# Feed-forward layer with 4-bit weights: the down projection's weights are prepared beside the gate and up products and kept in DRAM

## The reference

```python
w = stack([W_q >> 4 & 15, W_q & 15])               # two nibbles per word
w = (w - zero) * scale                             # one zero and scale for 64 inputs
x = x + layernorm(attention(layernorm(x)))
h = silu(layernorm(x) @ Wg.T) * (layernorm(x) @ Wu.T)   # inner width 2752
x = x + layernorm(h @ Wd.T)
```

## Time and profile before

| | us |
|---|---|
| median of 3 runs (2841.08 to 2845.24) | 2843.83 |
| the profiled execution's own time | 2843.78 |
| its span, first to last instruction | 2842.0 |
| PE busy | 2642.1 (93%) |
| DVE, ACT, POOL busy | 1573.4, 954.5, 1220.0 |
| gate and up: first to last matmul | 1462.7 to 2281.3 |
| down: first to last matmul | 2321.8 to 2829.1 |

### The profile page before, as it was taken

The page is one execution under the profiler, slowest core; times in us unless marked ns, Lnnn a source line. Parts: engine busy times, 40 slices in busy tenths (PEclk is TensorE's granted clock), DMA queues, the critical chain, the costliest instruction groups (busy, mean ns, idle before and its releaser), DMA issues. The chain is left out here.

```text
span 2842.0 us, 42348 instructions
## 1 busy us (share of the span) xinstructions
PE 2642.1 (93%) x17064; PEld 1116.6 (39%) x17064; DVE 1573.4 (55%) x1946; ACT 954.5 (34%) x1674; POOL 1220.0 (43%) x678
## 2 busy tenths in 40 slices
PE   6999899999999999989959989999999948499998
PEld 3445433333333333224424434444444413244443
DVE  6332777778778787525677686555555535300001
ACT  3111366666666666640112232222222211100000
POOL 0000277777777777742234434444444335300001
PEclk8999999999999999999979999999999979799999
DMA  4223101101011010022232122222222164323220
GB/s 168 76 78 91 29 17 31 42 16 29 20 40 29 16 29 1 1 82 97 103 88 62 52 55 75 75 74 75 74 75 75 37 195 134 113 85 123 69 69 30
DMA packets 200861, 187.16 MB, mean 66 GB/s; under 512 B 22512, under 2 KB 175600, under 8 KB 200688
## 3 DMA queue, kind: packets, MB, share of 16 engines
q1 hardware_dynamic: 188880, 177.02, 20.3%
q10 hardware_dynamic: 11808, 7.73, 1.0%
HBM read 134.74 MB, written 49.81 MB: 65 GB/s over the span
## 5 line engine op out<-in xcount | busy, mean ns | idle before, releaser
L728 POOL TENSOR_TENSOR c_prob<-c_prob 128x1024 f32<-128x1024 f32 (+1 forms) x288 | 605.1, 2120 | 517.8 <-ACT c_prob L626 515.2
L642 DVE TENSOR_REDUCE c_maxes<-c_s 128x2 f32<-128x1024 f32 (+3 forms) x640 | 645.7, 1058 | 196.1 <-PE c_s L482 196.1
L626 ACT ACTIVATE c_prob<-c_s 128x512 f32<-128x512 f32 (+1 forms) x1152 | 597.9, 571 | 299.3 <-PE c_s L504 185.3
L504 PE MATMUL c_s<-c_q,c_k 97*128 97x512 f16 (+3 forms) x1280 | 366.7, 352 | 10.1 <-ACT c_prob L626 1.7
L1182 PE MATMUL e_ps<-x_hi,e_w_hi 128*128 128x512 f16 x832 | 316.6, 381 | 16.1 <-DVE e_w_lo L1236 16.1
L1183 PE MATMUL e_ps<-x_lo,e_w_hi 128*128 128x512 f16 x832 | 316.6, 380 | 0.0
L1184 PE MATMUL e_ps<-x_hi,e_w_lo 128*128 128x512 f16 x832 | 316.4, 380 | 0.0
L1676 PE MATMUL f_yp<-f_wd_hi,f_h_hi 128*128 128x512 f16 x704 | 222.4, 383 | 84.5 <-DVE f_wd_lo L1738 76.9
L519 PE MATMUL c_ctx<-c_prob,v_sb 128*32 128x512 f32 (+3 forms) x2560 | 293.4, 539 | 0.2 <-ACT c_c L615 0.2
L1312 DVE TENSOR_TENSOR e_sums<-e_ps,e_sums 128x512 f32<-128x512 f32 x238 | 164.0, 689 | 229.3 <-PE e_ps L1184 227.7
L504 PEld LDWEIGHTS c_s<-c_q,c_k 97*128 97x128 f16 x1280 | 111.1, 97 | 345.2 <-ACT c_prob L626 298.7
(11 more groups left out here) (167 smaller groups left out, 3511.1 us busy)
## 6 DMA issues: line engine op xcount, KB each, us to landing
h_hi<-e_hh SPq DMA_DIRECT2D x84, 128.0 KB, 1.8
h_lo<-e_hl SPq DMA_DIRECT2D x84, 128.0 KB, 1.7
b_x<-L_attn_x SPq DMA_DIRECT2D x16, 512.0 KB, 6.1
c_q<-qk_hi SPq DMA_DIRECT2D x64, 128.0 KB, 3.1
d_x<-L_attn_x SPq DMA_DIRECT2D x16, 512.0 KB, 5.0
x_dram<-d_x SPq DMA_DIRECT2D x16, 512.0 KB, 2.6
out<-f_z SPq DMA_DIRECT2D x8, 1024.0 KB, 5.3
f_h_hi<-h_hi SPq DMA_DIRECT2D x6, 1344.0 KB, 8.5
```

Source lines behind the costliest of these rows:

```text
L504: last = nc.tensor.matmul(S2[:, h % 2, at:at + w], K[:, g % 2, k * P:(k + 1) * P], Q[:, g % 2, b, h, q:q + w], start=True, stop=not diag)
L626: nc.scalar.activation(prob(g, s, 0, w)[:, h, :], S2[:, h % 2, 0:w], ACT.Exp, scale=exp_scale).then_inc(exp_done, 1)
L642: last = nc.vector.tensor_reduce(MAXES[:, g % 2, t // TPB, heads, t % TPB, u], S1[:, heads, at:at + w], AX.X, ALU.max)
L728: return nc.gpsimd.tensor_tensor(one, one, two, ALU.add)
```

## The change

- The down weights are no longer prepared in the down stage. They become 24 more tasks of the gate and up stage (kind `DOWN`), one beside the first half of every pair but the sixth, in the second place of `W`, and two beside each half of the last pair. ACT and DVE cut them into the new tiles `DH` and `DL` (`cut_down`), and SP stores these to DRAM (`store_down`, `wd_hi` and `wd_lo`, 11.3 MB together).
- The down stage loads them: ACT's queue in six parts, of 1, 2, 3, 4, 6 and 5 chunks and the rest, SP's queue the first round's `h` in the same parts. PE takes chunk by chunk for the first 16 chunks, then 6 chunks tile by tile as before.
- The zeros and scales of a gate or up task come in one transfer each, from tables that are laid out for it beforehand (`by_run`), so that a task is 3 transfers.
- A joined tile is written where silu or `gated` reads it (`summed_in`, in `SILU` or `H`), and the ring goes. `SUMS` has 3 slots and no longer 6. T1 to T4 use these and `S`.
- The rest pair is third, and no longer fifth. T1 to T3 are made one piece at a time beside pairs 1 and 2, none beside the rest, and two pieces beside each half of the fourth pair. The fifth pair takes its products in the order 12, 22, 11, 21, and so waits for W2 at its second product.

```diff
     PLAIN = 5
-    pairs = [("gate", 0), ("up", 0), ("gate", 2), ("up", 2), ("rest", FULL)]
+    pairs = [("gate", 0), ("up", 0), ("rest", FULL), ("gate", 2), ("up", 2)]
     pairs += [(kind, c) for c in range(4, FULL - 1, 2) for kind in ("gate", "up")] + [("both", FULL - 1)]
...
+            task_no[q + 1, p] = len(tasks)
+            put(u, (q + 1, p) + tasks_of(q + 1)[p])
+        places = [1] if p == 0 and q + 1 < PAIRS and q != PLAIN else [0, 1] if q + 1 == PAIRS else []
+        for place in places:
+            number = sum(1 for t in tasks if t[2] == DOWN)
+            if number < len(downs):
+                down_in.setdefault(u, []).append(number)
+                put(u, (None, place, DOWN, number))
...
         if role(q) == "rest":
-            return ["2", "1"]
-        return ["P1", "P6", "P7", "P5", "P2", "P4", "P3"] if fast(q) else ["11", "12", "21", "22"]
+            return ["1", "2"]
+        if fast(q):
+            return ["P1", "P6", "P7", "P5", "P2", "P4", "P3"]
+        return ["12", "22", "11", "21"] if q == PLAIN - 1 else ["11", "12", "21", "22"]
...
+    made_beside = {(0, 0): [(0, 0)], (0, 1): [(0, 1)], (1, 0): [(0, 2)], (1, 1): [(0, 3)], (2, 0): [], (2, 1): [],
+                   (3, 0): [(1, 0), (1, 1)], (3, 1): [(1, 2), (1, 3)]}
...
-        SUMS = sb("sums", [P, 6, BANK])
+        SUMS = sb("sums", [P, 3, BANK])
+        DH, DL = sb("dh", [P, 2, BANK], F16), sb("dl", [P, 2, BANK], F16)
...
+        def summed_in(u, name):
+
+            q, p = u
+            if name in silus(q):
+                return SILU[:, p, silu_slot(name), :]
+            return H[:, (h_no[u + (name,)] - 1) % 2, :]
...
-                    for r in range(P // RUN):
-                        part = slice(r * RUN, (r + 1) * RUN)
-                        for table, dst in ((zeros, ZEROS), (scales, SCALES)):
-                            of_run = table.rearrange("(j r) i -> r j i", j=JC)[r:r + 1, :, cols]
-                            sp.dma_start(dst[part, slot, :].rearrange("p (j i) -> p j i", j=JC)[:, :, into],
-                                         of_run.broadcast_to([RUN, JC, width])).then_inc(raw_loaded[slot], 16)
+                    sp.dma_start(RAW[:, slot, :].rearrange("p (j i) -> p j i", j=JC),
+                                 words.rearrange("(j p) i -> p j i", p=P)[:, :, at * P:(at + 1) * P]
+                                 ).then_inc(raw_loaded[slot], 16)
+                    for table, dst in ((zeros, ZEROS), (scales, SCALES)):
+                        sp.dma_start(dst[:, slot, :], table[:, at * BANK:(at + 1) * BANK].unsqueeze(1)
+                                     .broadcast_to([P // RUN, RUN, BANK])).then_inc(raw_loaded[slot], 16)
...
+                for k in beside.get(u, []):
+                    if k + 2 < len(tasks):
+                        load(k + 2)
+                for number in down_in.get(u, []):
+                    store_down(number)
...
-                    if row and col == 0:
+                    if row:
                         pe.wait_ge(cut_lo, cut_no[q, "W2"])
...
+                if k >= AT_START:
+                    dve.wait_ge(cut_lo, cut_no[unit_of[k][0], weight_cuts(unit_of[k][0])[-1]])
+                earlier = [t[3] for t in tasks[:k] if t[2] == DOWN and t[1] == i]
+                if earlier:
+                    dve.wait_ge(down_lo, earlier[-1] + 1)
...
+            def cut_down(number):
+                n, planes = rows_of_words(tasks[down_task[number]])
+                i = tasks[down_task[number]][1]
+                dve.wait_ge(down_hi, number + 1)
+                if number:
+                    dve.wait_ge(down_lo_stored, 16 * number)
+                nc.vector.scalar_tensor_tensor(DL[0:n, 0:planes, :], W[0:n, i, 0:planes, :], WS, DH[0:n, 0:planes, :],
+                                               ALU.mult, ALU.subtract).then_inc(down_lo, 1)
...
+                    out = summed_in(u, name)
+                    if key in silu_waits and silu_waits[key]:
+                        dve.wait_ge(h_done, silu_waits[key])
+                    if key in h_no and h_no[key] > 2:
+                        dve.wait_ge(lo_done, h_no[key] - 2)
...
+                    for n, (of, j) in enumerate(made_beside[u]):
+                        make_t1_t2(of, j)
+                        cut_t(of, 1, j)
+                        cut_t(of, 2, j)
+                        gated(u, names[n])
+                        cut_t(of, 3, j)
+                    for name in weight_cuts(q + 1)[p:p + 1]:
                         cut(q + 1, name)
-                    for name in names[1:]:
+                    for number in down_in.get(u, []):
+                        cut_down(number)
+                    for name in names[len(made_beside[u]):]:
                         gated(u, name)
                 else:
                     gated(u, names[0])
+                    cut(q + 1, weight_cuts(q + 1)[p])
...
+            def cut_down(number):
+                k = down_task[number]
+                n, planes = rows_of_words(tasks[k])
+                act.wait_ge(scaled, k + 1)
+                if number:
+                    act.wait_ge(down_hi_stored, 16 * number)
+                    act.wait_ge(down_lo, number)
+                nc.scalar.activation(DH[0:n, 0:planes, :], W[0:n, tasks[k][1], 0:planes, :], ACT.Copy, scale=WS
+                                     ).then_inc(down_hi, 1)
...
+            for i, (first, end) in enumerate(parts):
+                for u in range(2):
+                    for buf, src in ((H_HI, h_hi), (H_LO, h_lo)):
+                        sp.dma_start(buf[:, u, first:end, :], src[first * P:end * P, rows(0, u)]
+                                     .rearrange("(c p) t -> p c t", p=P)).then_inc(part_loaded[i], 16)
+                        if end == FULL:
+                            sp.dma_start(buf[0:REST, u, FULL, :], src[FULL * P:, rows(0, u)]
+                                         ).then_inc(part_loaded[i], 16)
+            for u in range(2):
+                sp.dma_start(X[:, u], x1_dram[rows(0, u), :].rearrange("(s p) d -> p s d", p=P)
+                             ).then_inc(x_loaded[u], 16)
...
+                for i, (first, end) in enumerate(parts):
                     if c == first:
-                        pe.wait_ge(part_loaded[i], 64 * (2 if i == len(parts) - 1 else 1))
+                        pe.wait_ge(w_loaded[i], 16 * (4 if end == FULL else 2))
+                        pe.wait_ge(part_loaded[i], 16 * (8 if end == FULL else 4))
 
             def first_round():
-                for k, (m, half) in enumerate(tasks[:2 * APART]):
-                    if half == 0:
-                        arrived(2 * m)
-                    pe.wait_ge(cut_lo, k + 1)
+                for c in range(APART):
+                    arrived(c)
                     for u in range(2):
                         for s in range(2):
-                            for c in chunks_of(m):
-                                part_product(u, s, c, [half])
-                pe.wait_ge(cut_lo, len(tasks))
+                            part_product(u, s, c)
+                arrived(APART)
+                pe.wait_ge(cleared, 1)
                 for u in range(2):
...
-                    unpack(k + 1)
-                cut(k)
...
+                for buf, src in ((wd_hi, w_hi), (wd_lo, w_lo)):
+                    act.dma_start(buf[:, first:end, :], src[first * P:end * P, :].rearrange("(c p) d -> p c d", p=P)
+                                  ).then_inc(w_loaded[i], 16)
+                    if end == FULL:
+                        act.dma_start(buf[0:REST, FULL, :], src[FULL * P:, :]).then_inc(w_loaded[i], 16)
...
+def by_run(table):
+
+    inter = table.shape[1]
+    runs = table.reshape(4, 4, inter)
+    return [runs[:, :, at:at + P].transpose(1, 0, 2).reshape(4, -1) for at in range(0, inter, P)]
```

More of the change, by code:

```diff
@@ L1150, in _ @@
             for u in units:
-                if u in prepared and prepared[u] + 2 < len(tasks):
-                    load(prepared[u] + 2)
+                for k in beside.get(u, []):
[3 more added lines that the diff above has]
+                    store_down(number)
                 q, p = u
@@ L1329, in plain @@
                     gated(u, names[0])
+                    cut(q + 1, weight_cuts(q + 1)[p])
                     for j in (2 * p, 2 * p + 1):
                         make_t4(0, j)
[L1332 removed]
                     gated(u, names[1])
+                    for number in down_in.get(u, []):
+                        cut_down(number)
+                    gated(u, names[2])
                     for j in (2 * p, 2 * p + 1):
@@ L1378, in _ @@
             for u in units:
-                if u in prepared:
-                    unpack(prepared[u])
+                for k in beside.get(u, []):
+                    unpack(k)
                 (strassen if fast(u[0]) else plain)(u)
@@ L1540, in _ @@
                 q, p = u
-                if u in prepared:
```

(11 more changed lines are left out.)

334 lines of the change are left out of this document (138 added, 196 removed).

## The result

The changed kernel takes 2796.38 us (median of 4 runs, 2792.37 to 2798.05) against 2844.53: a ratio of 0.983, with a 95% interval of 0.9813 to 0.9847. It is faster by 48 us. The forecast was 2773 us, in a range of 2764 to 2785, so the sign was right and the size wrong: 71 us of gain were counted and 48 came. The profiled execution took 2792.37 us, 51.4 less than that of before, and 19.3 more than the sum of 2773.1.

What follows compares the result with a forecast made beforehand. PE, busy 2642.1 of 2842.0 us, was taken as the bound, leaving some 200 us to win. Gains of 27.5 + 37 + 4.5 + 1.7 = 70.7 us from 2843.8 gave 2773 us, 8-in-10 range 2764 to 2785.

Steps and rivals of the forecast that it cites:

- The first round: Down stage's first round: no more waits for weights, 118.9 us instead of 155.8, gain 37 us, between 32 and 42.
- second rival: Down stage's first round: queues alternate packets, so short-packet `h` arrives late; 5 to 7 us more, 2779 us; 15%.
- The start: Start of gate and up: the first task's last table is issued 2.9 us sooner; gain 1.7 us, between 0 and 3.
- 256 KB and lands in 4.7 us: First gate or up task: its last table transfer is 256 KB and lands in 4.7 us, not 2.1.
- The gap: PE idle between the stages: two ACT and four SP transfers replace unpacking; gain 27.5 us, between 25 and 29.5.
- the last pair's double tasks: Last pair: a second `cut_down` waits about 2 us for the first one's store; price 0, at most 3.
- The plain pairs: Pairs before the Strassen pairs: the 12.4 us stall before P6 goes, a fifth-pair stall comes; gain 4.5 us.
- 7.9 are lost: Fifth pair's second product: W2 is cut at 73.2, 5.9 us late, plus some 2 us of slow clock.
- third rival: Fifth pair's stall at its upper bound, or a second at the first Strassen pair's P7: 6.5 us more, 2780; 10%.
- The down tasks beside Strassen pairs: Strassen pairs: DVE's idle time absorbs each task's work; price 0, or 38 us if all reached W2.
- fourth rival: Strassen pairs wait for DVE's late W2 cut: milder forms 2785 to 2840 us, 4%; slower than before, 2850, 2%.
- a bound for the down load's landing (7 us): Gap between the stages: if the down load lands in 7 us, the gain is 25 us instead of 27.5.

Runs made afterwards that it cites:

- sixteen rows: The changed kernel with each table row four times in DRAM, one transfer reading 16 rows for 8 partitions each: 2779.74 us, ratio 0.9781.
- the moved tasks: Against sixteen rows, the down tasks beside pairs three to five go to the second units of pairs nine to eleven: 2774.35 us, ratio 0.9757.
- three orders: sixteen rows alone, 2779.74 us; the changed kernel with W2's cut between the fourth pair's pieces, 2793.13; sixteen rows with both W2 cuts earlier, 2781.58.
- a fourth: Against sixteen rows, the rest pair is fifth again, with one piece of T1 to T3 beside each plain unit: 2782.66 us, ratio 0.9791.
- less beside POOL: Against sixteen rows, POOL's T3 sums beside the fourth pair cover 8 of 512 columns, useful for times only: 2770.28 us in one run.
- W2 ahead of the moved tasks: sixteen rows, both W2 cuts earlier, down tasks moved, last pair's planes in turn; W2 also cut before the moved tasks' unpacking: 2769.57 us, ratio 0.9735.

## Why the prediction was right or wrong, point by point

- **The first round (37 us): right, a little low.** 116.4 us against 118.9, with one wait of 0.62 us for `h`. The second rival, `h` starved by its short packets, cost 0.62 us at most: 165 GB/s were moved, and but for that wait the first 16 chunks arrived ahead of PE. Its direction was right: in the second part 128 KB of `h_lo` landed 9.1 us after its issue and 512 KB of `wd_lo` after 6.8, and both waits of PE here, 19.6 and 0.62, ended with `h_lo`. No run varies the packets.
- **The start (+1.7 forecast, -5.3 measured): wrong.** The step that failed is "256 KB and lands in 4.7 us": I took the landing of a transfer with 128 rows at its source for one with four. It is 8.4 us. With sixteen rows the landing is 4.4, and the start 19.3, which is 0.5 better than before and not 1.7. The term was also added up wrongly: an issue 2.9 us sooner and a landing of 4.7 in place of 2.1 leave 0.3 us and not 1.7. Less 3.7 for the landing and some 1.7 for the second task's scales, that is the -5.3 to within 0.2.
- **The gap (27.5 us forecast, 20.9 measured): half wrong.** The 6.4 us from the first issue to PE came true (6.5). What failed is the last pair's double tasks: "a second `cut_down` waits for the first one's store, about 2 us", priced "0, at most 3". The wait was 13.6 us, because the store is queued behind tables that together keep the DMA engines busy for 0.13 of their time. It was not at the side of the path either: DVE's lag moved PE's next stage by about 6 us.
- **The plain pairs (4.5 us forecast, -5.9 measured with the rest of gate and up): right at the fifth pair but for the size, and wrong in what comes behind it.** Pieces of 10.6 and 8.4 (8.6 measured), a second half of 22.4 (22.6) and a stall at the fifth pair's second product came true. W2 came at 78.4 and not 73.2. Of the 5.2 us, 3.8 are DVE's start at the fourth pair: 26.8 us behind PE's start of the rest and not 23, since the rest's two units hold a down task and two waits for ACT (3.3 and 4.4 us), which I had not written out. 1.2 are the first half (29.0, not 27.8). The step that failed is "7.9 are lost", one stop and then none: a backlog of DVE that I followed to one product did not end there. PE waited 1.7 us at P7 of the sixth pair and 2.3 at P7 of the eighth, the latter gone with sixteen rows, and it ran at 1.2 GHz for 3 to 5 us behind the first and the last of the three stops. The third rival had this form, a longer stall or one at P7, at 10%; it holds in part.
- **The down tasks beside Strassen pairs (0): nearly right where they stood.** In the 480 us from 1720 PE is idle for 2.3 us, and for none with sixteen rows. It is not free in general, as the moved tasks show: with W2's cut behind a task in the same unit PE waits up to 4.7 us. The measured 2796 us lie where the fourth rival had its milder forms (2785 to 2840), but its mechanism, W2 late in pair after pair, gives at most the 2.3 us of the eighth pair.
- **Shares of the error of 24.0 us in the first three terms** (the round gives 2.5 back). Sixteen rows take 5.8 of 7.0 at the start, 4.7 of 10.4 in gate and up and 5.0 of 6.6 in the gap: the shape of one transfer is 15.5 us of it, and the spans agree: 2790.5 us against 2777.2, in which the last transposes came 2.8 us later, so 16.1. What is left, 8.5 us, is mostly gate and up (5.7): 13.0 us of waits in two places where I had 5.9 in one. By the medians' ratios (0.983 and 0.9781) sixteen rows are worth 13.9 us.
- **The range** took in only unknowns inside each term's mechanism; none of its ends had a table that lands late. I had a bound for the down load's landing (7 us) and none for the tables', though the merging of transfers was the part of the change that altered a shape.

## What to carry to other kernels

When several transfers become one, write down the outermost dimension of both sides before any landing time is carried over: here 4 in place of 16 cut the rate from 289 to 100 GB/s, and it delayed even the stores queued behind it. When a stall on a busy engine is moved by reordering, add up all the stalls behind it until the engine is idle again: with three orders the sum in pairs five to seven stayed at 12 to 13 us, a fourth made it 15.9, and only less work there (or less beside POOL) made it smaller. Where the engine has time left, order does help: W2 ahead of the moved tasks took 1.6 us of waits and the slow clock behind them. A double use of a single buffer costs as long as the slowest thing that can stand ahead of its store.
